# A transformer layer on eight cores: a wait before every counted operation, LayerNorm's last step on GpSimd, earlier weight loads and a deeper attention look-ahead

## The reference

```
x = x + attn_a(layernorm(x))   # 16 heads, blocks of 64 tokens and 8 global tokens
x = x + ffn(layernorm(x))      # router: best 2 of 8 experts, and 2 shared experts, hidden 512
x = x + attn_b(layernorm(x))   # 16 query heads, 4 KV heads, causal, ALiBi slopes
x = x + ffn(layernorm(x))      # the same weights again

layernorm: (x - mean) / sqrt(var + 1e-5)
expert:    (silu(x @ w1) * (x @ w3)) @ w2
attn_b:    q = x @ Wq.T; k, v = split(x @ Wkv.T)
           softmax(q @ k.T / 8 + slope * (key - query), causal) @ v, then @ Wo.T
```

## Time and profile before

| what | value |
|---|---|
| time of the runs | 8320.50 and 8916.32 us, median 8618.41 us |
| the profiled execution's own time | 8319.44 us |
| its span on the slowest core (core 7) | 8317.9 us |
| spans of the 8 cores | 8257.2 to 8317.9 us |
| TensorE matmul busy | 6412.3 us, 77% of the span |
| VectorE busy | 2320.2 us, 28% |
| ScalarE busy | 1778.0 us, 21% |
| GpSimd busy | 380.7 us, 5% (only the issue of transfers) |

### The profile page before, as it was taken

The page is one execution under the profiler, slowest core; times in us unless marked ns, Lnnn a source line. Parts: engine busy times, 40 slices in busy tenths (PEclk is TensorE's granted clock), DMA queues, the critical chain, the costliest instruction groups (busy, mean ns, idle before and its releaser), DMA issues.

```text
span 8317.9 us, 94217 instructions; the slowest of 8 cores (8257.2 to 8317.9 us)
## 1 busy us (share of the span) xinstructions
PE 6412.3 (77%) x32824; PEld 3038.5 (37%) x32824; DVE 2320.2 (28%) x5754; ACT 1778.0 (21%) x2914; POOL 380.7 (5%) x702
## 2 busy tenths in 40 slices
PE   0198988967988779885677777778759887888788
PEld 0044444433433334332233334434434333333333
DVE  0033333332233222322533222121222322233222
ACT  0011111110111001110134544645641100111010
POOL 1000000000000000000000000000000000000000
PEclk9977677679999999997665555555559999999999
DMA  9700010023333333333000000000013343433333
GB/s 118 96 21 21 21 41 21 11 92 132 132 140 143 133 140 123 142 144 103 20 32 3 19 21 21 1 21 11 1 51 117 142 147 132 148 116 147 130 138 122
DMA packets 167315, 689.34 MB, mean 83 GB/s; under 512 B 14512, under 2 KB 45360, under 8 KB 125904
## 3 DMA queue, kind: packets, MB, share of 16 engines
q0 software_dynamic: 132880, 548.84, 21.4%
q1 hardware_dynamic: 33984, 134.48, 4.5%
HBM read 661.59 MB, written 98.60 MB: 91 GB/s over the span
## 4 chain that ended last, share of the span: by engine, by line
PE 69%; DMA 8%; DVE 8%; issue 6%; another core or an unknown queue 4%; ACT 3%; DVEq 1%; ACTq 0%; SPq 0%; POOLq 0%
PE pf L1021 14%; PE pf L1030 13%; PE pf L1307 10%; PE pf L1093 8%; DMA f_w2s<-ffw 6%; PE pf L412 5%; PE pf L1347 4%; PE pf L432 3%; PE pf L611 1%; PE pb L389 1%; ACT b_PT L1330 1%; PE pf L740 1%; DVE xn L381 1%; PE pf L745 1%
## 5 line engine op out<-in xcount | busy, mean ns | idle before, releaser
L1093 PE MATMUL pf<-f_w2s,f_H1G 128*128 128x512 bf16 x5120 | 1159.2, 383 | 237.5 <-DMA f_w2s<-ffw 178.9
L1021 PE MATMUL pf<-xnT,f_w1s 128*128 128x512 bf16 x5120 | 1222.8, 382 | 0.0
L1030 PE MATMUL pf<-xnT,f_w3s 128*128 128x512 bf16 x5120 | 1209.5, 379 | 0.3
L1330 ACT ACTIVATE b_PT<-pf,alibi_sb 128x512 bf16<-128x512 f32 (+3 forms) x1657 | 1017.5, 621 | 729.8 <-PE pf L1307 592.6
L1307 PE MATMUL pf<-b_QT,b_Kz 128*128 128x512 bf16 (+3 forms) x1657 | 854.4, 516 | 248.0 <-DVE b_Vaug L1236 0.7
L1093 PEld LDWEIGHTS pf<-f_w2s,f_H1G 128*128 128x128 bf16 x5120 | 488.8, 98 | 907.9 <-issue 373.6
L1040 ACT ACTIVATE f_sA<-pf 128x512 bf16<-128x512 f32 x640 | 382.7, 598 | 1753.2 <-PE pf L1021 1752.8
L1347 PE MATMUL pf<-b_Vaug,b_PT 128*128 128x65 bf16 x5565 | 615.1, 244 | 162.1 <-ACT b_PT L1330 151.4
L1030 PEld LDWEIGHTS pf<-xnT,f_w3s 128*128 128x128 bf16 x5120 | 500.4, 98 | 605.9 <-issue 19.9
L1021 PEld LDWEIGHTS pf<-xnT,f_w1s 128*128 128x128 bf16 x5120 | 493.2, 98 | 608.3 <-issue 44.6
L1048 DVE SCALAR_TENSOR_TENSOR f_t<-pf,f_sA 128x512 bf16<-128x512 f32 x512 | 354.3, 692 | 1046.4 <-PE pf L1030 1004.5
(11 more groups left out here) (186 smaller groups left out, 4549.1 us busy)
## 6 DMA issues: line engine op xcount, KB each, us to landing
f_w1s<-ffw POOLq DMA_DIRECT2D x160, 1024.0 KB, 5.6
f_w3s<-ffw POOLq DMA_DIRECT2D x160, 1024.0 KB, 7.9
f_w2s<-ffw POOLq DMA_DIRECT2D x320, 512.0 KB, 3.8
Xa<-xout SPq DMA_DIRECT2D x16, 2048.0 KB
xf<-Xa SPq DMA_DIRECT2D x16, 2048.0 KB
xf<-x SPq DMA_DIRECT2D x8, 2048.0 KB
ffw<-f_w POOLq DMA_DIRECT2D x16, 1024.0 KB, 46.8
Xb<-xout SPq DMA_DIRECT2D x8, 2048.0 KB
```

Source lines behind the costliest of these rows:

```text
L1021: slot=slot: t.matmul(pA_["t"][:, 0:CH], w1s[:, sl, ic, 128 * hc:128 * hc + 128], xnT[slot][:, ic, :], start=(ic == 0), stop=(ic == 7)),
L1030: slot=slot: t.matmul(pB_["t"][:, 0:CH], w3s[:, sl, ic, 128 * hc:128 * hc + 128], xnT[slot][:, ic, :], start=(ic == 0), stop=(ic == 7)),
L1093: pos=pos, a_=accs[j]: t.matmul(a_["t"][:, 0:512], H1G[:, e, hc, 128 * j:128 * j + 128], w2s[:, sl, hc, :], start=(pos == 0 and hc == 0), ...
L1330: j0=j0, pS=pS: s.activation(PTs[ki % 4][:, j0:qc], pS["t"][:, j0:qc], AF.Exp, bias=alibi_sb[:, col:col + 1]),
```

## The change

There are five edits.

1. Every counted operation now waits first for its own engine's previous counted operation.
2. In `ln_chunk` the four operations that write `xn` go from VectorE to GpSimd, with the waits that belong to them (for rstd, for the transposes of the previous LayerNorm, for the loaded rows). TensorE waits for GpSimd's count, and the load that refills `xf` waits for GpSimd too.
3. In `attn_b` the load of Wkv goes to a region of its own, the third quarter of `Kz`, and is issued right behind that of Wq, ahead of Wq's transposes.
4. `load_transpose` takes a region and a load that is already issued.
5. In the loop over key blocks, b_pv is held back until more than three blocks are pending, instead of two.

```diff
@@ class K, op
-            boundary = not self._had_wait[e]
+            boundary = True
@@ ln_chunk
             k.wait("y", "v", bufm.get(("xf_v", slot), 0))
+            k.wait("y", "g", bufm.get(("xf_g", slot), 0))
...
-            k.wait("v", "s", m_rstd)
-            k.wait("v", "t", bufm.get("xn_t", 0))
+            k.wait("g", "s", m_rstd)
+            k.wait("g", "t", bufm.get("xn_t", 0))
+            k.wait_dma("g", mld)
             for j in range(NT):
-                k.op("v", lambda v, j=j: v.tensor_scalar(
+                k.op("g", lambda g_, j=j, slot=slot: g_.tensor_scalar(
                     xn_sb[:, j, :], xf[slot][:, j, :], mv[:, j, 0:1], rstd[:, j:j + 1],
                     ALU.subtract, ALU.mult), inc=(j == NT - 1))
-            m_xn = k.cnt["v"]
-            k.wait("t", "v", m_xn)
+            m_xn = k.cnt["g"]
+            bufm[("xf_g", slot)] = m_xn
+            k.wait("t", "g", m_xn)
@@ attn_b, load_transpose
-                def load_transpose(nat_src, n_oc, evac_plan):
-                    k.wait("g", "t", k.cnt["t"])
-                    mldw = k.dma("g", wnat[:, 0:n_oc, :], nat_src)
+                def load_transpose(nat_src, n_oc, evac_plan, region=None,
+                                   preloaded=None):
+                    region = wnat if region is None else region
+                    if preloaded is None:
+                        k.wait("g", "t", k.cnt["t"])
+                        mldw = k.dma("g", region[:, 0:n_oc, :], nat_src)
+                    else:
+                        mldw = preloaded
                     k.wait_dma("t", mldw)
+                    wnat_ = region
...
-                mwq = load_transpose(ab_Wq.rearrange("(a p) i -> p a i", p=128), 8, wq_plan)
+                wkv_region = Kz[:, 2:3, :].rearrange("p a (b d) -> p (a b) d",
+                                                      b=S // D)[:, 0:4, :] \
+                    if S >= 4 * D else None
+                mq_pre = k.dma("g", wnat[:, 0:8, :],
+                               ab_Wq.rearrange("(a p) i -> p a i", p=128))
+                mkv_pre = (k.dma("g", wkv_region[:, 0:4, :],
+                                 ab_Wkv.rearrange("(a p) i -> p a i", p=128))
+                           if wkv_region is not None else None)
+                mwq = load_transpose(None, 8, wq_plan, preloaded=mq_pre)
...
-                mwkv = load_transpose(ab_Wkv.rearrange("(a p) i -> p a i", p=128), 4, wkv_plan)
+                if wkv_region is not None:
+                    mwkv = load_transpose(None, 4, wkv_plan, region=wkv_region,
+                                          preloaded=mkv_pre)
...
@@ attn_b, loop over key blocks
-                                if len(pend) > 2:
+                                if len(pend) > 3:
                                     b_pv(*pend.popleft())
```

More of the change, by code:

```diff
@@ L1161, in load_transpose @@
                             b = bpool.acquire()
[L1162 to L1165, removed]
+                            k.op("t", lambda t, a=a, icb=icb, b=b, wnat_=wnat_:
+                                 t.matmul(
+                                     b["t"][:, 0:128],
+                                     wnat_[:, a, 128 * icb:128 * icb + 128],
+                                     idn_bf[:], start=True, stop=True,
+                                     is_transpose=True), inc=True)
                             b["wmark"] = k.cnt["t"]
@@ L1183, in wkv_plan @@
                             (wkvV[:, icb, 64 * a:64 * a + 64], 64, 128)]
-                mwkv = load_transpose(ab_Wkv.rearrange("(a p) i -> p a i", p=128), 4, wkv_plan)
+                if wkv_region is not None:
+                    mwkv = load_transpose(None, 4, wkv_plan, region=wkv_region,
+                                          preloaded=mkv_pre)
+                else:
+                    mwkv = load_transpose(ab_Wkv.rearrange("(a p) i -> p a i", p=128),
+                                          4, wkv_plan)
                 def wo_plan(a, icb):
```

## The result

The changed kernel takes 8.15% longer: a ratio of 1.0815 to the kernel before, with a 95% interval of 1.0785 to 1.0844. The fastest execution took 8976.2 us against 8307.3 us, some 670 us more. I had forecast 386 us more, and a range that ended at 8900 us. The direction was right and the size was not.

The account below looks back on a forecast made before the run. TensorE, busy 77% of the span, was taken to bound the kernel. Terms 199 + 28 + 25 - 30 - 10 + 97 + 62 + 21 - 6 = +386 us on 8319.4 gave 8705 us, range 8500 to 8900.

Parts of the forecast that it names:

- xn on GpSimd: All 32 LayerNorms: TensorE waits for four xn at 1.5 us each on GpSimd, +97 us (0 to 289).
- the load term: FFN stages: w1 and w3 loads queue behind xn on GpSimd, so TensorE waits 4.4 us 14 times, +62 us.
- GpSimd is far slower: Rival on the LayerNorms' xn: 3.0 us each, +289 for +97, total 8897 us; chance 0.08.
- stop in the PV run: attn_b steady step: the fourth PV matmul waits for the score matmul, 0.17 us in 1173 runs, +199 us.
- L1010 and TensorE's stops in FFN: FFN: the gate broadcast matmul waits for the preceding group's end, 128 x 0.22 us, +28; other group matmuls nothing.
- VectorE's and ScalarE's stops: Attention tile ends: masked exponentials, PV runs and token transposes get self-wait stops, +25 us (0 to 60) for 168 tiles.
- look-ahead: attn_b tile ends: three score-exponential pairs in flight cover part of PV's wait for exponentials, -30 us (0 to 151.4).
- Wkv beside Wq: attn_b weight transposes: Wkv's load runs under Wq's, removing TensorE's 10.0 us idle, -10 us.
- w1 and w3 behind xn, clock, w2: FFN: expert loads delayed behind xn +62, low clock after the pause +21, less pressure on the last w2 load -6.
- PV stop free: Rival in attn_b: only the stop in the PV run costs nothing, all else as summed, 8506 us; chance 0.13.
- look-ahead pays: Rival in attn_b: the stop doesn't bite and look-ahead removes all 151.4 us of exponential waits, 8385 us; chance 0.08.
- whole run held: Rival in attn_b: the score must end before the first PV matmul, +211 more, 8916 us; chance 0.03.

Follow-up runs that it names:

- e4: Kernel before with only xn moved to GpSimd, plus the unconditional self-wait on GpSimd alone: 8779.3 us against 8307.3.
- e7: Kernel before with the unconditional self-wait on TensorE only: 8493 us in its faster execution, 186 over before.
- e8: Kernel before with the unconditional self-wait on VectorE and ScalarE only: whole span 107 us over before.
- e1: Changed kernel with the four xn operations back on VectorE, all other edits kept: ratio 1.0264 to the kernel before.
- e3: Kernel before with only the deeper look-ahead in attn_b: 75 us less than before on the mean.
- e2: Kernel before with only the self-waits, on all engines: 282 us more than before on the mean.
- b1: Kernel before with the look-ahead of three, the early Wkv load and each xn counted; old waits, xn on VectorE: ratio 0.9916.
- e5: e4 with the first two experts' w1 and w3 loads issued ahead of the next LayerNorm: span 396 us over before, FFN stages 59 shorter than e4.
- b2: b1 with the LayerNorm cut into steps so its transposes stand later in TensorE's queue: ratio 0.9579 to the kernel before, 7938 us at best.
- e6: e4 with seven forms of GpSimd operations added behind the layer's end; whole time means nothing; xn form 3776 ns, copy 1038 ns.

## Why the prediction failed, step by step

The step that failed is the term "**xn on GpSimd**". I had no row of GpSimd computing, took 1.5 us per operation as "a plain one-element-at-a-time rate" and 3.0 as the upper bound, which was VectorE's slowest row doubled. It is 3.77. With it the same working gives 32 x (15.1 - 2.98) = +388 us instead of +97; measured in attn_b were 8 x 12.1, and e4 less the load term makes 448 - 59 = 389. This one term is 291 us too small, and the whole miss was 284. The mechanism (TensorE stands still, VectorE's freed time buys nothing, four operations in a row) was right, and the rival "GpSimd is far slower" named it, with 0.08 for its chance; its price was too low because the bound came from another engine. A row of VectorE bounds nothing on GpSimd. I should have kept the upper end open, or made it as wide as a ratio of several.

The Trainium skill, GPSIMD Engine Reference, section Performance versus the Vector engine, gives 1.96 for the ratio of the engines, on a two-input sum; here the measured ratio for L381's form is 3773 / 808 = 4.7, so its figure doesn't carry over to this form. Its section Engine selection calls one-input operations roughly line-rate. Of the forms here only the copy comes near it, with 1038 ns for 1024 columns; the one-input tensor_scalar took 2841 and 3776 ns. The measurement decides.

The other terms, by size. Their sum came out well (289 forecast, 266 measured), but that is luck, since errors of both signs cancelled:

| term | forecast | measured | from |
|---|---|---|---|
| stop in the PV run | +199 | +163 | e7, attn_b |
| L1010 and TensorE's stops in FFN | +28 | +21 | e7, both FFN stages |
| VectorE's and ScalarE's stops | +25 | +98 | e8 |
| look-ahead | -30 | -66 | e1 less e7, e8 and the next line, in attn_b (e3 itself: -55 in attn_b, -75 by span) |
| Wkv beside Wq | -10 | -9 | e1 against e2, b1 against before, stretch of the weight transposes |
| xn on GpSimd | +97 | +389 | e4 less the next line |
| w1 and w3 behind xn, clock, w2 | +62 +21 -6 | +59 | e5 against e4 |
| sum | +386 | +655 | 669 between the fastest executions, 661 between the mean spans |

- *PV stop.* The fourth matmul starts 0.15 later, not 0.17: the rows of S and PV are each rounded and modelled, and the step is 1.10 instead of 1.12. The stage shows a little less than the steps (163 of 171). The rivals "PV stop free", "look-ahead pays" and "whole run held" all fall by that row.
- *Small stops.* I held that "other VectorE and ScalarE operations wait for TensorE anyway". At the tile ends of attn_b they don't: there masks, exponentials and the last PV runs form a chain of their own, 168 times, and a stop in it delays TensorE; 46 us of growth in the wait for exponentials stand there and in the short tiles. Nor do they at the weight transposes (11 us), which the prediction left out. I priced the whole at 25, within a range of 0 to 60, and it was 98 (107 by span). The 28 us of it in the FFN stages and the 16 in attn_a were not traced to a place.
- *L1010.* TensorE's idle before it grew from 54.2 to 78.6 us over its 128 matmuls in e7, so 24 of the 28 us are there, 0.19 each.
- *Wkv.* The 9 to 11 us of waiting for its load are gone, and that is what it pays. With the new self-waits the stretch from the first weight transposes to the first projections takes 102.0 us in e1 and 111.0 in e2; without them 87.0 in b1 and 96.7 in before (core 0 of each). In after (101.6) the gain is hidden, because the self-waits make the same stretch 14 us longer.
- *w3.* 5.4 us of waiting for each of 14 chunks in after, 4.6 in e4, against 4.4 forecast. What GpSimd's queue holds back showed as worked out from the code.
- *Clock.* No separate price could be read: e5 took away the wait with its clock effect and gained 59 in all, 18 less than the three terms.

The parts don't add up to the last microsecond. e4's attn_a is 117 us longer; it holds nine of the 32 LayerNorms (the first one of ffn is emitted at its end), so 9 x 12.1 = 109 are explained. By whole spans e2, e3, Wkv and e4 give 282 - 75 - 9 + 455 = 653 of the 661; but e1 has 223 where e2, e3 and Wkv give 198, so the parts change each other by some 25 us, and that stays open.

## What to carry to other kernels

An operation moved to an idle engine costs its whole duration there if a third engine stands waiting for it; look first whether the waiting engine can be given other work (b2 against b1: the same operations, the transposes later in TensorE's queue, gained 3.4%), and only then whether the operation can move. A duration on an engine that computes nothing in the profile can't be bounded by another engine's rows: measure one operation of the exact form, or leave the range open. And a wait that is added everywhere is priced at the few places where a chain crosses engines in short steps, not only in the steady loop.

## What the hardware showed that I had not expected

- GpSimd's two-operation tensor_scalar costs 3.33 ns per column of 128 partitions; at 1024 columns it takes 4.7 times VectorE's time, while its copy of the same data with conversion takes 1.04 us, 3.6 times less (e6). One arithmetic operation less saves a quarter (2841 against 3776 ns).
- A matmul that waits for the end of the previous counted one starts 0.15 us after it, and within a run of four of 0.244 us each this adds 0.15 us to the run, with no larger gap behind it (after and e7).
- VectorE's and ScalarE's own stops add up to 98 us in this kernel (e8) without changing its steady step of 0.95 us.
